# Attention stage with three banks for transposed probabilities, and feature products added up in the bank of attended values

## The chip, the cores and the metric

One core of one Trainium2 chip runs the whole program. The metric is the device time of one execution in microseconds. The kernel before took 2473.31 us (median of 3 runs, 2469.48 to 2473.86). Engines are called TensorE (PE in the profile; PEld is its weight load), VectorE (DVE), ScalarE (ACT), GpSimd (POOL) and SyncE (SP, which here only issues DMAs).

## The reference

x is 16 batch rows of 512 tokens with 128 values. Each row is layer-normalised, then `x + attention(xn) + ffn(xn)` is returned. The change lies wholly in the attention, which has 16 heads of width 8 and learned relative positions, clipped at 20 on both sides:

```python
idx = clip(pos[None, :] - pos[:, None], -20, 20) + 20
attn1 = einsum('bhqd,bhkd->bhqk', q, k)
attn2 = einsum('bhqd,qkd->bhqk', q, rel_k[idx])
attn = softmax((attn1 + attn2) / sqrt(8), axis=-1)
w1 = einsum('bhqk,bhkd->bhqd', attn, v)
w2 = einsum('bhqk,qkd->bhqd', attn, rel_v[idx])
out = (w1 + w2).transpose(0, 2, 1, 3).reshape(B, S, E) @ Wo.T + bo
```

w2 is computed from "features": for each query and head the probabilities of the 40 keys near it, as a 640-long vector, times a table made of rel_v. The second half of the sum, a small attention and a mixture of experts, is done by the two later stages, which the change leaves as they are.

## The kernel before, in words

Three stages follow each other: `attend`, `mix` and `experts`. Each is a block in which every engine runs its own list of instructions, written out by hand; engines meet at semaphores only. `attend` goes over 16 batch rows, and preparations for a row (normalising, q, k, v, splits into bf16 parts) are made two rows ahead (LEAD = 2) between the work of the row in hand.

A row has 16 **units** (u = 0 to 15). A unit has 4 score tiles of 128 x 512 (each for 32 queries of each of 4 heads), treated as two pairs. For a pair, TensorE makes the scores (L469) in the four-bank tensor b_s, VectorE adds the relative-position window (L644) and takes the negated maximum (L679), and ScalarE takes the exp with its sum (L818). One unit later TensorE transposes each tile of probabilities (L481, four products of 128 x 128 per tile) into one of two banks, b_pt. ScalarE reads tiles 0 and 2 (L792), VectorE tiles 1 and 3 (L661) into SBUF. Three units later TensorE multiplies them with v (L502, 16 instructions a unit) into the bank b_o, where the four 128-column quarters belong to the four tiles of 128 queries (t = u // 4). Per pair TensorE's order is scores, then (in the second pair) attended, then the transposes of the pair (`row`, L546 to 575).

The banks b_pt also take other jobs. JOBS (L74 to 78) lists all of them in order of unit; `bank_of` (L104) gives a job the bank of its index modulo 2, and `bank_free`, `job_done` and `job_read` (L217 to 227) count, from that list, what has to have happened before. So every job waits until the job two places before it has been read out. The other jobs are, after the four tiles of their unit:

- units 0, 4, 8, 12: `features` (L508): four transposes of feature chunks into one bank, the fifth into the next. ScalarE copies the four to feat_t (L830), VectorE the fifth to last_t (L701).
- units 3, 5, 6, 13: x transposed (L437, read at L755), q (L440, read by VectorE at L612), k (L440, read at L760) and v (L443, read at L782) of the row that is prepared.
- units 10, 11, 14, 15: the products with the relative-position table ("qr", L451), in two banks, read by ScalarE (L737, L738). The first waits for both banks (L447, L448).
- unit 9: the output product of the row before (L542, read at L836 and L715).

`weigh` (L522) multiplies the features with the table in units 1, 5, 9 and 13, for the features of t = (u // 4 - 2) % 4, so that t = 2 and 3 of a row fall into units 1 and 5 of the next. It uses a bank of its own, b_w. ScalarE copies b_o to o_sb in unit 2 of the next row (L824). When the fourth weigh is done, VectorE adds b_w to o_sb in unit 6 (L709, 128 x 512). Then GpSimd's `scale` (L989) adds the part of the far keys and multiplies by the inverse sums (L993, L995), GpSimd goes on with the row's next features (L906 to L926), and TensorE makes the output product in unit 9. In row 0, 20 warm-up products go to b_w in unit 3 (L563).

A start flag on a matmul clears the marks of its bank in the partitions that it writes; a product without the flag overwrites where the mark is clear and adds where it is set. Before, `attended` sets the flag on the first products of each quarter (hh == 0), and `weigh` on its first chunk. The file holds these flags as

```python
first = hh == 0
ins = nc.tensor.matmul(b_w[:, 0, t * P:(t + 1) * P], feat_w[:, c, :], ..., start=c == 0, stop=c == FC - 1)
```

Of the kernel before, what the change touches and what calls it, by code (L numbers as in the profile page):

```python
# [72 lines left out]
LEAD = 2  # L73
JOBS = [(u, "probs", j) for u in range(UNITS) for j in range(NJ)]  # L74
JOBS += [(u, "features", n) for u in range(0, UNITS, 4) for n in range(2)] + [(9, "out", n) for n in range(2)]
# [4 lines left out]
OF_ROW_BEFORE += [(9, "out", n) for n in range(2)]  # L80
# [14 lines left out]
def jobs_before(b, job, bank=None):  # L95

    def count(jobs):
        return sum(bank is None or JOBS.index(x) % 2 == bank for x in jobs)

    earlier = JOBS[:JOBS.index(job)]  # L100
    return sum(count(OF_ROW[n]) for n in range(-LEAD, b)) + count([x for x in earlier if x in OF_ROW[b]])


def bank_of(job):  # L104
    return JOBS.index(job) % 2
# [8 lines left out]
def attend(nc, w, scr):  # L114
# [11 lines left out]
    with ExitStack() as ctx:  # L126
# [52 lines left out]
        b_pt = [ps(f"pt{n}") for n in range(2)]  # L179
        b_o, b_w = ps("o"), ps("w")  # L180
# [13 lines left out]
        pt_ps, pt_ev = sem("pt_ps"), [sem("pt_ev0"), sem("pt_ev1")]  # L194
        av_ps, w_ps, o_ev, w_ev = sem("av_ps"), sem("w_ps"), sem("o_ev"), sem("w_ev")
# [224 lines left out]
        def _(pe):  # L420
# [65 lines left out]
            def attended(b, u, s):  # L486

                t, hh = u // 4, u % 4
# [7 lines left out]
                first = hh == 0  # L496
# [25 lines left out]
            def weigh(b, u):  # L522

                t = (u // 4 - 2) % NT
                for n in range(2):
                    job_read(pe, b, (u - 1, "features", n))
                if t == 0:
                    need(pe, w_ev, b, 1, 0)
                for c in range(FC):
                    ins = nc.tensor.matmul(b_w[:, 0, t * P:(t + 1) * P], feat_w[:, c, :],  # L530
                                           feat_t[:, c, :] if c < FC - 1 else last_t[:, t, :],
                                           start=c == 0, stop=c == FC - 1)
                ins.then_inc(w_ps, 1)
# [12 lines left out]
            def row(b, s, m, first=False, tail=False, lead=False):  # L546
# [5 lines left out]
                for u in range(10 if tail else UNITS):  # L552
                    if u == 0 and not tail:
                        pe.wait_ge(qk_in[s], m * QK_IN + QK_IN)
                    for pair in ((0, 1), (2, 3)):
                        if not tail:
                            scores(b, u, pair, s)
                        if pair[0]:
                            if u > 2 and not tail:
                                attended(b, u - 3, s)  # L560
                                if first and u == 3:

                                    warm_up(nc, b_w[:, 0, 0:P], ident[:], WARM)  # L563
                            elif u < 3 and not first:
                                attended(b - 1, u + UNITS - 3, 1 - s)
                        for j in pair:
                            if (u and not tail) or (u == 0 and not first):
                                transpose(b, u, j)
                    if u % 4 == 1 and not (first if u < 8 else tail):
                        weigh(b, u)  # L570
# [11 lines left out]
        def _(v):  # L582
# [81 lines left out]
            def row(b, s, m, first=False, tail=False, lead=False):  # L664
# [4 lines left out]
                for u in range(10 if tail else UNITS):  # L669
# [24 lines left out]
                    if u % 4 == 0 and not (first if u < 8 else tail):  # L694
                        job = (u, "features", 1)
                        t = (u // 4 - 2) % NT
                        job_done(v, b, job)
                        if t == 0:
                            need(v, w_ps, b, NT, 0)
# [5 lines left out]
                    if u == 6 and not first:  # L705

                        v.wait_ge(w_ps, b * NT)
                        v.wait_ge(o_ev, b)
                        nc.vector.tensor_tensor(o_sb[:], o_sb[:], b_w[:, 0, :].rearrange("p (t q) -> p t q", q=P),  # L709
                                                ALU.add).then_inc(w_ev, 1)  # L710
# [14 lines left out]
        def _(act):  # L725
# [69 lines left out]
            def row(b, s, m, first=False, tail=False, lead=False):  # L795
# [6 lines left out]
                for u in range(10 if tail else UNITS):  # L802
# [23 lines left out]
                    if u % 4 == 0 and not (first if u < 8 else tail):  # L826
                        job = (u, "features", 0)
                        job_done(act, b, job)
                        need(act, w_ps, b, NT, u // 4 - 2)
# [14 lines left out]
        def _(g):  # L844
# [144 lines left out]
            def scale(b):  # L989

                g.wait_ge(w_ev, b)
# [778 lines left out]
```

## Time and profile before

| what | value |
|---|---|
| median of 3 runs | 2473.31 us (2469.48 to 2473.86) |
| the profiled execution | 2466.72 us, its span 2464.9 us |
| TensorE busy | 2128.0 us (86%) |
| VectorE busy | 1864.7 us (76%) |
| ScalarE busy | 1619.9 us (66%) |
| GpSimd busy | 1030.4 us (42%) |
| DMA engines in the first stage | 54% |
| mean granted clock of TensorE | 0.961 |

The profile is of one execution. Busy time is the union of an engine's instructions; the time just before an instruction in which its engine was idle is shown in brackets, with what ended it. Instructions of the same kind that follow each other are merged into one line of the timeline with their count. The page's own chain of waits runs back from the end of the program and stays in the last stage, so it says nothing on the first.

### The profile page before, as it was taken

The numbers are of one execution on the slowest core, as the hardware profiler recorded it, in microseconds if no ns is written. First come the engines' busy times: TensorE is split into PE (matmuls) and PEld (weight loads), VectorE is DVE, ScalarE is ACT, GpSimd is POOL, SyncE is SP. The second block draws the span as 40 slices with busy tenths as digits, with TensorE's granted clock in tenths as the row PEclk, the third lists the DMA queues.
The fourth block names the chain that finished last, engine by engine and source line by source line (L and its number), as shares of the span: only waits on it lengthen the run. The fifth ranks groups of instructions, "written<-read, shape, count | busy, mean of one in ns | idle before, by whom it ended". The sixth has DMA issues, their size and how long they took to land. (4 is left out here: it accounts for less than half of the span.)

```text
span 2464.9 us, 77225 instructions
## 1 busy us (share of the span) xinstructions
PE 2128.0 (86%) x27816; PEld 1444.4 (59%) x27816; DVE 1864.7 (76%) x4151; ACT 1619.9 (66%) x4178; POOL 1030.4 (42%) x1270
## 2 busy tenths in 40 slices
PE   3388888888888888888888888599999978999999
PEld 1266566666666666666666666356666645666665
DVE  1388888888888888888888889367676756877777
ACT  2288888888888888888888878367777752323222
POOL 4246655655656656556655554200000003333332
PEclk7699999999999999999999999789999998999999
DMA  3355655555655655555555554200100110010110
GB/s 101 104 123 130 149 137 120 148 134 121 149 130 127 147 136 129 140 134 128 144 134 125 136 119 83 46 23 26 39 26 26 38 61 26 30 35 26 32 32 18
DMA packets 571232, 228.63 MB, mean 93 GB/s; under 512 B 465590, under 2 KB 543030, under 8 KB 566326
## 3 DMA queue, kind: packets, MB, share of 16 engines
q1 hardware_dynamic: 570934, 224.63, 36.8%
q8 instruction: 191, 3.13, 0.5%
q14 instruction: 107, 0.88, 0.1%
HBM read 129.61 MB, written 94.90 MB: 91 GB/s over the span
## 5 line engine op out<-in xcount | busy, mean ns | idle before, releaser
L818 ACT ACTIVATE a_probs<-a_bank_s,a_neg_max 128x512 f32<-128x512 f32 x1024 | 695.0, 685 | 134.0 <-DVE a_neg_max L679 131.0
L679 DVE TENSOR_REDUCE a_neg_max<-a_bank_s 128x2 f32<-128x1024 f32 x512 | 627.1, 1225 | 55.6 <-DVE a_bank_s L644 1.9
L481 PE MATMUL a_bank_pt<-a_ident,a_probs 128*128 128x128 f32 x4096 | 588.2, 284 | 64.8 <-ACT a_feat_t L830 42.9
L481 PEld LDWEIGHTS a_bank_pt<-a_ident,a_probs 128*128 128x128 f32 x4096 | 444.1, 143 | 201.0 <-issue 67.5
L792 ACT ACTIVATE a_probs_t<-a_bank_pt 128x512 f32<-128x512 f32 x512 | 306.0, 598 | 138.7 <-PE a_bank_pt L481 136.9
L661 DVE COPY a_probs_t<-a_bank_pt 128x512 f32<-128x512 f32 x512 | 349.7, 683 | 26.9 <-PE a_bank_pt L481 21.9
L502 PE MATMUL a_bank_o<-a_probs_t,a_v 128*32 128x128 f32 x8192 | 285.4, 281 | 1.4 <-issue 0.2
L644 DVE TENSOR_TENSOR a_bank_s<-a_bank_s,a_win 128x144 f32<-128x144 f32 (+2 forms) x640 | 161.3, 271 | 148.2 <-PE a_bank_s L469 145.3
L1537 ACT ACTIVATE e_gate<-e_bank_g 128x512 f32<-128x512 f32 x144 | 85.9, 597 | 273.9 <-PE e_bank_g L1476 273.9
L502 PEld LDWEIGHTS a_bank_o<-a_probs_t,a_v 128*32 128x32 f32 x8192 | 215.0, 112 | 58.1 <-issue 39.6
L937 POOL TENSOR_TENSOR a_win<-a_raw,a_band 128x1152 f32<-128x1152 f32 x64 | 168.9, 2639 | 105.2 <-issue 73.8
L1484 PEld LDWEIGHTS e_bank_y<-e_w,e_hid 128*128 128x128 f32 x1152 | 149.4, 192 | 95.2 <-issue 56.5
L818 ACT ACTIVATION_READ_ACCUMULATOR a_probs<-a_bank_s,a_neg_max 128x1 f32 x1024 | 203.7, 199 | 0.0
L1226 DVE TENSOR_REDUCE m_neg_max<-m_bank_s 128x2 f32<-128x1024 f32 x128 | 156.7, 1225 | 60.3 <-PE m_bank_s L1190 53.1
L1323 ACT ACTIVATE m_probs<-m_bank_s,m_neg_max 128x512 f32<-128x512 f32 x256 | 173.5, 683 | 13.4 <-DVE m_neg_max L1226 5.0
L469 PE MATMUL a_bank_s<-a_kl,a_q 48*32 48x204 bf16 (+14 forms) x3840 | 156.1, 275 | 20.3 <-ACT a_probs L818 20.0
L1199 PEld LDWEIGHTS m_bank_pt<-m_ident,m_probs 128*128 128x128 f32 x1024 | 112.4, 143 | 99.0 <-issue 82.7
L1289 POOL TENSOR_TENSOR m_rms<-m_rms,m_pows 128x4 f32<-128x4 f32 x16 | 16.1, 1008 | 368.8 <-DVE m_rms L1239 368.8
L1484 PE MATMUL e_bank_y<-e_w,e_hid 128*128 128x128 f32 x1152 | 156.0, 279 | 16.0 <-DVE e_hid L1646 16.0
L469 PE MATMUL a_bank_s<-a_k,a_q 48*32 48x512 bf16 (+15 forms) x4096 | 166.0, 289 | 0.0
L451 PE MATMUL a_bank_pt<-a_relx,a_t 64*128 64x320 f32 x256 | 62.1, 503 | 112.0 <-DVE a_probs_t L661 64.8
L1561 DVE SCALAR_TENSOR_TENSOR e_y<-e_bank_y,e_comb,e_y 128x128 f32<-128x128 f32 x512 | 143.9, 344 | 12.2
(163 smaller groups left out, 3489.7 us busy)
## 6 DMA issues: line engine op xcount, KB each, us to landing
scr_probs<-a_probs SPq DMA_DIRECT2D x512, 72.0 KB, 2.4
a_raw<-scr_qr SPq DMA_DIRECT2D x256, 96.0 KB
scr_qr<-a_qr SPq DMA_DIRECT2D x64, 320.0 KB, 3.6
a_feat<-scr_probs SPq DMA_DIRECT2D x256, 78.0 KB, 2.4
scr_parts<-a_sp SPq DMA_DIRECT2D x144, 128.0 KB, 2.4
a_left<-scr_probs SPq DMA_DIRECT2D x256, 64.0 KB, 2.5
a_q<-scr_parts SPq DMA_DIRECT2D x32, 192.0 KB
a_k<-scr_parts SPq DMA_DIRECT2D x32, 192.0 KB
```

Of the source, the lines that this page charges most:

```text
L469: ins = nc.tensor.matmul(b_s[g * QBLK:(g + 1) * QBLK, p, a:z], Q[s][par:par + ROWS, half, at:at + QBLK], keys[s][par:par + ROWS, half, a:z ...
L481: ins = nc.tensor.transpose(b_pt[bank_of(job)][:, 0, t * P:(t + 1) * P], probs[(u - 1) % 4][:, j, MAX_REL + t * P:MAX_REL + (t + 1) * P], ...
L502: ins = nc.tensor.matmul(out, V[s][:, V_SLOTS.index((edge, kt)), j, hh * 24:hh * 24 + 32], blocks[:, :, :, kt * P + j * QBLK:kt * P + (j + ...
L644: ins = nc.vector.tensor_tensor(near, near, bass.AP(own.tensor, own.offset, [own.ap[0], [step, n], [1, z - a]]), ALU.add)
L661: nc.vector.tensor_copy(probs_t[(u - 1) // 2 % 2][:, spot(u - 1, PLACES[j]), :], b_pt[bank_of(job)][:, 0, :]).then_inc(pt_ev[bank_of(job)], 1)
L679: nc.vector.tensor_reduce(neg_max[:, 2 * pair:2 * pair + 2], b_s[:, 2 * pair:2 * pair + 2, :], AX.X, ALU.max, negate=True).then_inc(max_ok, 1)
L792: nc.scalar.activation(probs_t[(u - 1) // 2 % 2][:, spot(u - 1, PLACES[j]), :], b_pt[bank_of(job)][:, 0, :], ACT.Copy).then_inc(pt_ev[bank ...
L818: nc.scalar.activation(probs[u % 4][:, j, MAX_REL:MAX_REL + S], b_s[:, j, :], ACT.Exp, bias=neg_max[:, j:j + 1], accum_out=sums[:, t, PLAC ...
L937: nc.gpsimd.tensor_tensor(win[t % 2][:], over, band[:].rearrange("p (o h c) -> p o h c", o=1, h=1) .to_broadcast([P, NQB, NJ, WIN]), ALU.m ...
L1226: nc.vector.tensor_reduce(neg_max[:, 2 * pair:2 * pair + 2], b_s[:, 2 * pair:2 * pair + 2, :], AX.X, ALU.max, negate=True).then_inc(max_ok, 1)
L1323: nc.scalar.activation(probs[:, j, :], b_s[:, j, :], ACT.Exp, bias=neg_max[:, j:j + 1], accum_out=sums[s][:, u, j:j + 1]).then_inc(exp_ok, 1)
L1484: ins = nc.tensor.matmul(b_y[k][:, t * P:(t + 1) * P], hid[k][:, t * P:(t + 1) * P], w2[:, e, :], start=True, stop=True)
```

## The change

The feature products of t = 0, 1 and 2 are added straight into b_o, in the quarter of their tile, with no start flag; only the very first attended products of a row (u == 0) have one. The products of t = 3 come when b_o already takes the next row; they go, as a new job WEIGHED at unit 5, to one of the b_pt banks, and VectorE adds that 128 x 128 part to o_sb at the end of unit 5. b_w is gone, and b_pt has three banks, given by the job's index modulo 3. ScalarE's guard on feat_t and GpSimd's guard in `scale` follow. The warm-up products go to b_o at the end of unit 2 of row 0.

```diff
 LEAD = 2
+PT_BANKS = 3
+WEIGHED = (5, "weigh", 0)
...
-JOBS += [(u, "features", n) for u in range(0, UNITS, 4) for n in range(2)] + [(9, "out", n) for n in range(2)]
+JOBS += [(u, "features", n) for u in range(0, UNITS, 4) for n in range(2)] + [WEIGHED] + [(9, "out", n) for n in range(2)]
...
 def bank_of(job):
-    return JOBS.index(job) % 2
+    return JOBS.index(job) % PT_BANKS
...
-        b_pt = [ps(f"pt{n}") for n in range(2)]
-        b_o, b_w = ps("o"), ps("w")
+        b_pt = [ps(f"pt{n}") for n in range(PT_BANKS)]
+        b_o = ps("o")
...
-                first = hh == 0
+                first = u == 0
...
-                if t == 0:
-                    need(pe, w_ev, b, 1, 0)
+                apart = t == NT - 1
+                if apart:
+                    bank_free(pe, b, WEIGHED)
+                out = b_pt[bank_of(WEIGHED)][:, 0, 0:P] if apart else b_o[:, 0, t * P:(t + 1) * P]
                 for c in range(FC):
-                    ins = nc.tensor.matmul(b_w[:, 0, t * P:(t + 1) * P], feat_w[:, c, :],
-                                           feat_t[:, c, :] if c < FC - 1 else last_t[:, t, :],
-                                           start=c == 0, stop=c == FC - 1)
-                ins.then_inc(w_ps, 1)
+                    ins = nc.tensor.matmul(out, feat_w[:, c, :], feat_t[:, c, :] if c < FC - 1 else last_t[:, t, :],
+                                           start=apart and c == 0, stop=c == FC - 1, skip_group_check=True)
+                ins.then_inc(pt_ps if apart else w_ps, 1)
...
-                                if first and u == 3:
-
-                                    warm_up(nc, b_w[:, 0, 0:P], ident[:], WARM)
...
+                    if first and u == 2:
+                        warm_up(nc, b_o[:, 0, 0:P], ident[:], WARM)
...
+                        if t == 0 and not first:
+                            job_done(v, b, WEIGHED)
                         if t == 0:
-                            need(v, w_ps, b, NT, 0)
                             need(v, att_ok, b, 1, 0)
...
-                    if u == 6 and not first:
-
-                        v.wait_ge(w_ps, b * NT)
+                    if u == 5 and not first:
+                        job_done(v, b, WEIGHED)
                         v.wait_ge(o_ev, b)
-                        nc.vector.tensor_tensor(o_sb[:], o_sb[:], b_w[:, 0, :].rearrange("p (t q) -> p t q", q=P),
-                                                ALU.add).then_inc(w_ev, 1)
+                        nc.vector.tensor_tensor(o_sb[:, NT - 1, :], o_sb[:, NT - 1, :], b_pt[bank_of(WEIGHED)][:, 0, 0:P],
+                                                ALU.add).then_inc(pt_ev[bank_of(WEIGHED)], 1)
...
-                        need(act, w_ps, b, NT, u // 4 - 2)
+                        if u != 8:
+                            need(act, w_ps, b, NT - 1, {0: -1, 4: 0, 12: 1}[u])
+                        elif not first:
+                            job_done(act, b, WEIGHED)
...
-                g.wait_ge(w_ev, b)
+                g.wait_ge(o_ev, b)
+                job_read(g, b, WEIGHED)
```

## Rows read from the trace of the kernel before

**Rows 1.** The stretches view of four parts of the span; busy us per engine, clock, DMA.
```profile
98.00:1576.00 1478.00, 1267.60 (x21800) 912.48 (x21782) 1236.83 (x2558) 1180.09 (x3023) 828.88 (x1138) 0.98 0.54 129
```

**Rows 2.** VectorE's add at L709, one per batch row: first and last start.
```profile
L709 DVE TENSOR_TENSOR a_o_sb<-a_o_sb,a_bank_w x16: 676/676/689, 226.9 to 1567.8; 128x512 f32<-128x512 f32 x16
```

**Rows 3.** The stretches view of fifteen pieces of 89.4 us, from 98 us on.
```profile
187.40:276.80 89.40, 77.25 (x1357) 55.45 (x1358) 75.99 (x160) 73.52 (x190) 51.82 (x69) 1.00 0.57 136
276.80:366.20 89.40, 77.09 (x1308) 55.06 (x1307) 75.05 (x157) 72.32 (x186) 53.19 (x74) 0.98 0.56 138
...
sum 1341.00, PE 1156.26 PEld 829.89 DVE 1129.54 ACT 1086.81 POOL 770.69; mean PE 77.08 PEld 55.33 DVE 75.30 ACT 72.45 POOL 51.38
```

**Rows 4.** The waits view from 700 to 1060 us: us in total, times, longest.
```profile
PE a_bank_pt L451 <- DVE a_probs_t L661: 18.4, 16, 1.4
...
PE a_bank_pt L481 <- ACT a_feat_t L830: 10.3, 15, 0.7
...
PE a_bank_pt L515 <- ACT a_probs_t L792: 7.2, 15, 0.8
...
PE a_bank_s L469 <- ACT a_probs L818: 3.3, 11, 0.3
```

**Rows 5.** VectorE's groups of instructions from 833 to 923 us: busy, mean ns, idle before.
```profile
L679 DVE TENSOR_REDUCE a_neg_max<-a_bank_s 128x2 f32<-128x1024 f32 x32 | 39.2, 1225 | 3.4
...
L644 DVE TENSOR_TENSOR a_bank_s<-a_bank_s,a_win 128x144 f32<-128x144 f32 (+2 forms) x40 | 10.1, 271 | 6.7 <-PE a_bank_s L469 6.6 <-DVE a_y_in L715 0.2
...
L701 DVE COPY a_last_t<-a_bank_pt 128x128 f32<-128x128 f32 x4 | 1.2, 292 | 1.7 <-PE a_bank_pt L519 1.7
...
L612 DVE TENSOR_SCALAR a_t<-a_bank_pt,a_bias_q 128x512 f32<-128x512 f32 x1 | 0.8, 751 | 0.7 <-PE a_bank_pt L440 0.7
```

**Rows 6.** The timeline of all engines in unit 10: start, us, instruction, idle before.
```profile
799.04 1.09 PE L481 MATMUL a_bank_pt<-a_ident,a_probs 128*128 128x128 f32 x8
...
800.03 0.59 ACT L792 ACTIVATE a_probs_t<-a_bank_pt 128x512 f32<-128x512 f32 x1
...
800.73 0.68 DVE L661 COPY a_probs_t<-a_bank_pt 128x512 f32<-128x512 f32 x1
...
801.55 0.90 PE L451 MATMUL a_bank_pt<-a_relx,a_t 64*128 64x320 f32 x4 [1.42 <-DVE a_probs_t L661]
...
802.87 0.32 DVE L644 TENSOR_TENSOR a_bank_s<-a_bank_s,a_win 128x144 f32<-128x144 f32 x1 [1.46 <-PE a_bank_s L469]
```

**Rows 7.** The timelines of TensorE and VectorE around unit 12's features.
```profile
812.64 0.63 PE L515 MATMUL a_bank_pt<-a_ident,a_feat 128*128 128x128 f32 x4 [0.40 <-ACT a_probs_t L792]
...
814.75 1.09 PE L481 MATMUL a_bank_pt<-a_ident,a_probs 128*128 128x128 f32 x8 [0.70 <-ACT a_feat_t L830]
...
813.74 0.29 DVE L701 COPY a_last_t<-a_bank_pt 128x128 f32<-128x128 f32 x1 [0.42 <-PE a_bank_pt L519]
```

**Rows 8.** The timelines of TensorE and VectorE in units 3 to 6.
```profile
865.16 0.39 PE L530 MATMUL a_bank_w<-a_last_t,a_feat_w 128*128 128x128 f32 x2
...
870.77 1.13 PE L440 MATMUL a_bank_pt<-a_xnt,a_wk 128*128 128x512 f32 x2 [0.49 <-ACT a_probs_t L792]
...
855.13 0.32 DVE L644 TENSOR_TENSOR a_bank_s<-a_bank_s,a_win 128x144 f32<-128x144 f32 x1 [0.29 <-PE a_bank_s L469]
...
866.44 0.75 DVE L612 TENSOR_SCALAR a_t<-a_bank_pt,a_bias_q 128x512 f32<-128x512 f32 x1 [0.68 <-PE a_bank_pt L440]
...
871.42 0.68 DVE L709 TENSOR_TENSOR a_o_sb<-a_o_sb,a_bank_w 128x512 f32<-128x512 f32 x1
872.31 0.32 DVE L644 TENSOR_TENSOR a_bank_s<-a_bank_s,a_win 128x144 f32<-128x144 f32 x1 [0.22 <-PE a_bank_s L469]
```

**Rows 9.** GpSimd's timeline, the end of unit 8's feature chain.
```profile
880.42 0.22 POOL L926 TENSOR_TENSOR a_feat<-a_left 128x16 f32<-128x16 f32 x1
```

**Rows 10.** Stretches of 3 us, and TensorE's timeline, behind unit 14.
```profile
827.00:830.00 3.00, 3.00 (x44) 2.19 (x46) 2.54 (x5) 2.51 (x6) 1.88 (x2) 0.50 0.91 160
...
826.61 1.94 PE L481 MATMUL a_bank_pt<-a_ident,a_probs 128*128 128x128 f32 x8
```

More of the change, by code:

```diff
@@ L79 @@
 OF_ROW_BEFORE = [(0, "probs", j) for j in range(NJ)] + [(u, "features", n) for u in (0, 4) for n in range(2)]
-OF_ROW_BEFORE += [(9, "out", n) for n in range(2)]
+OF_ROW_BEFORE += [WEIGHED] + [(9, "out", n) for n in range(2)]
 def of_row(b):
@@ L97, in count @@
     def count(jobs):
-        return sum(bank is None or JOBS.index(x) % 2 == bank for x in jobs)
+        return sum(bank is None or bank_of(x) == bank for x in jobs)
     earlier = JOBS[:JOBS.index(job)]
@@ L193, in attend @@
         s_ps, max_ok, exp_ok = sem("s_ps"), sem("max_ok"), sem("exp_ok")
-        pt_ps, pt_ev = sem("pt_ps"), [sem("pt_ev0"), sem("pt_ev1")]
-        av_ps, w_ps, o_ev, w_ev = sem("av_ps"), sem("w_ps"), sem("o_ev"), sem("w_ev")
+        pt_ps, pt_ev = sem("pt_ps"), [sem(f"pt_ev{n}") for n in range(PT_BANKS)]
+        av_ps, w_ps, o_ev = sem("av_ps"), sem("w_ps"), sem("o_ev")
         p_out = [sem(f"p_out{k}") for k in range(4)]
```

## The prediction

> **What bounds the kernel now.** I read the stretches first, then the waits inside the attention stage, then short pieces of each engine's timeline.
>
> The change touches the first of three stages, from about 98 to 1576 us of a span of 2464.9 us [rows 1]; what follows has the same instructions before and after and only starts earlier. The 16 batch rows follow each other at (1567.8 - 226.9) / 15 = 89.4 us [rows 2]. Of such a stretch TensorE is busy 77.1 us, VectorE 75.3, ScalarE 72.5 [rows 3]. No engine is full; three engines hand 64 banks of transposed probabilities to each other in a row. So the reader has to ask, wait by wait, who is late.
>
> From 700 to 1060 us, which is 4.03 rows, the largest waits of TensorE are on the two pt banks [rows 4]: 16 waits of the products for the relative-position table (L451, "QR" below) on VectorE's copy of the last transposed tile, 18.4 us; 15 waits of the first transposes after the features on ScalarE's copy of the features, 10.3 us; 15 of the feature transposes (L515) on ScalarE's copy of a tile, 7.2 us. Per row that is 4.6 + 2.6 + 1.8 us; with the smaller ones of the same kind, for x, q and k, about 10.3.
>
> Not all of this is on the path. VectorE's idle time shows what is [rows 5]: in one row it waits 6.7 us ahead of the window add (L644), most of it in the second half of the row, 1.7 us ahead of the copy of the last feature chunk (L701), 0.7 ahead of the q copy (L612). Its 3.4 us ahead of L679 have no releaser: they are the delay from an add to the maximum of its result, 0.11 us each, and stay. In units 0 to 9 VectorE works almost without a gap, and TensorE's bank waits are mostly absorbed; in units 9 to 15 they are passed on to VectorE nearly one for one.
>
> **The change, part by part.** With three banks a job waits for the reader of the third job before it, not of the second. JOBS has 87 entries, a multiple of 3, so the rotation closes at each row and no job's wait on a pt bank gets stricter.
>
> **QR products, units 10, 11, 14, 15.** The first waits for both banks. Today the later of the two holds the last tile of the unit, read by VectorE; afterwards it holds the tile before, read by ScalarE. In unit 10 ScalarE ends at 800.03 + 0.59 = 800.62 us, VectorE at 800.73 + 0.68 = 801.41, and the products start at 801.55 [rows 6]: 0.79 us to gain, as TensorE's own transposes end before (799.04 + 1.09 = 800.13). The same subtraction gives 0.67, 0.83 and 0.53 us in units 11, 14 and 15: 2.8 us a row. VectorE then sits idle 1.46 us for the scores behind it [rows 6], so this is on the path. A part comes back: the second tile of the next unit now waits for ScalarE's read of the first QR bank, which stands behind two exps and hardly moves. Today both tiles wait for it, so the second half of that unit gains one tile's time, 1.09 / 2 = 0.54, where the first half gained 0.8. I take 0.6 each, **2.4 us a row** (ends 2.0 and 2.8).
>
> **Features, units 0, 4, 8, 12.** The four transposes need no ScalarE copy any more (they wait 0.40 us in unit 12), so the fifth, and with it VectorE's copy behind its 0.42 us of idle, comes about 0.4 us earlier [rows 7]. The first tile after them no longer waits 0.70 us for the feature copy; the second does, and gains 0.5. 0.45 each, **1.8 us a row** (ends 1.2, where VectorE's backlog absorbs a third, and 2.4).
>
> **x, k and the big add (units 3, 5, 6).** x: VectorE's 0.29 us of idle behind it [rows 8], **0.3**. At unit 6 today's add of 128x512 takes 0.68 us of VectorE, while TensorE's k product has waited 0.49 us for a bank, and VectorE then idles 0.22 us for the scores [rows 8]. Both leave together: **0.6** (ends 0.2 and 0.9). The new add of 128x128 stands at unit 5. Its price from the nearest row, the 128x128 copy from a bank, is 0.29 us [rows 7]. It waits for the weigh of the last tile, which ends at 865.16 + 0.39 = 865.55 us; VectorE idles 0.68 us until 866.44, for a q product that TensorE issues after the weigh anyway [rows 8]. So it costs nothing while that gap holds; without the cover it costs its 0.3 us and the wait for the weigh. Queued behind it are the q copy and the next window add.
>
> **At nothing.** The weigh products keep count and kind; whether start is on shows in no row as a difference, L502 has both. The v products (unit 13) and the output product (unit 9) come on TensorE right behind weigh, without a bank wait; VectorE's gaps there are TensorE's own work and stay. The warm-up moves up by about one unit in the first row only, at the same cost; I bound the effect at 2 us either way. GpSimd's scaling starts some 5 us earlier, as its releaser moves up from unit 6 to 5. Today the feature chain behind it ends at 880.42 + 0.22 = 880.64 us [rows 9], about when TensorE could transpose: it would be late next in a faster row, and is relieved. After that comes the load of left, which in the three other places leaves several us. SyncE's queue issues the same DMAs in the same order.
>
> **The clock.** Once in most rows TensorE's granted clock falls to 0.50 (1.2 GHz; elsewhere 2.4) for some 3 us, right after unit 14's QR wait [rows 10]: 8 transposes take 1.94 us instead of 1.09, and a full 3 us at half speed is 1.5 us of work lost. 11 of the 15 stretches stand at 0.98, three at 1.00 [rows 3]. If all dips go that is 17 us; if none, 0. The wait ahead of them shrinks to under 0.5 us, but unit 10's longer wait has no dip behind it, so the wait alone doesn't decide. I take 10 us.
> The Trainium skill ("TensorE: Matmul & The Clock Gate", section "A second HAM failure mode: psum-queue depth-cycling") blames small idle gaps of TensorE between groups for such a clock. By it all dips would go, 17 us in place of 10; the trace agrees on their place, not on which gap brings them.
>
> **Sum.** 2.4 + 1.8 + 0.3 + 0.6 = 5.1 us a row. x, k and QR are there in the 14 rows that prepare another: 71 us. The two last rows have features and add only: 2 x 2.3 = 5. The stage's tail has the add on its last chain, 0.68 against 0.3: 0.4. With the clock's 10: 86 us. The profiled execution took 2466.7 us around its span of 2464.9; the median of three runs is 2473.3, 0.3% more, and I take the difference over to it: **2387 us**.
>
> **The rivals.**
> *A, VectorE and ScalarE set the pace.* What TensorE gains comes back as waits on exps, of which it has 3.3 us in 4.03 rows today [rows 4]: ScalarE has the QR reads and the splits on top of its exps in units 10 to 15. Then half of QR (1.2) and the features of three units (0.4 x 3) stay, and 0.5 for the add: 2.9 x 14 + 5 = 45 us, 2428 us. For it: units 0 to 9 are like that. Against: the 6.7 us that VectorE waits are on TensorE's scores, not on ScalarE. Chance 0.22.
> *B, all bank waits go.* 10.3 us a row in 14 rows, 144 us: 2329 us. Against: VectorE's idle time is no longer than that, and part of it is TensorE's own work. Chance 0.09.
> The Trainium skill ("Perfetto Trace Analysis", section "Optimizing Tensor Performance") says to rotate independent groups through banks so that evacuation overlaps the next group. Taken alone it gives B.
> *C, no change.* The banks are not the limit: the QR products start a fixed delay after the transposes. Rows 6 speak against it, with 1.42 us between. 2473 us, chance 0.05.
> *D, slower: the clock.* TensorE gets ahead of VectorE, works in short bursts, waits on exps, and the clock falls more often. A dip costs 1.5 us: from 5.1 / 1.5 = 3.4 extra dips a row on, the gain is gone. With five more a row it loses 7.5 - 5.1 = 2.4 us in 14 rows, 34, less the last rows' 5: 2502 us. Against: in units 0 to 9 TensorE waits on exps already, and one whole row holds 1.00 [rows 3]. Chance 0.05.
> *Forecast:* chance 0.59.
>
> **How the numbers follow.** About 0.2%, 5 us, is what a measurement of this kernel can tell from no change. Forecast, A and B are on the fast side: 0.90; C 0.05; D 0.05. The forecast's own bounds: low ends 2.0 + 1.2 + 0.2 + 0.2 = 3.6 a row, 50 + 5, clock 0: 55 us, 2418; high ends 2.8 + 2.4 + 0.3 + 0.9 = 6.4, 90 + 5 + 17: 112 us, 2361. The range goes down to 2345, halfway to B, and up to 2432, over A; left out are C, D and most of B, under 0.2.
>
> **What would show it.** The pitch of the rows down from 89.4 to about 84 us. The QR products released by ScalarE's copy (L792) after under 0.7 us, no more by L661. No wait of the feature transposes for a tile copy; the wait for the feature copy on the second tile, near 0.1 us. VectorE's idle ahead of the window add near 4 us a row instead of 6.7. The 128x128 add without idle that outlasts the weigh. More stretches at 1.00. It would be wrong if TensorE's scores waited on exps by 3 us a row (A), or if stretches at 0.50 multiplied (D).

## The result, and the profile after

The kernel after took 2433.09 us (median of 4 runs, 2432.04 to 2443.62), the kernel before beside it 2471.39 us (4 runs, 2469.14 to 2473.86). The ratio is 0.9854, 95% interval 0.9825 to 0.9884: 38 us gained where 86 were forecast, and 1 us outside the range. The profiled execution of after is the slowest of its four, 2443.6 us, so its trace shows 23 us less than the profiled one of before.

The stretch of the first stage, and the small add that ends each row's sum, both of the kernel after:

```profile
98.00:1553.00 1455.00, 1260.99 (x21800) 921.34 (x21784) 1225.48 (x2560) 1154.80 (x3024) 829.30 (x1138) 0.96 0.55 131
```

```profile
L712 DVE TENSOR_TENSOR a_o_sb<-a_o_sb,a_bank_pt x16: 227/230/287, 217.9 to 1543.9; 128x128 f32<-128x128 f32 x16
```

The row pitch is (1543.9 - 217.9) / 15 = 88.4 us, against 89.4 [rows 2] and 84.3 forecast. The granted clock of the stage is 0.96, against 0.98 [rows 1]. The two later stages take 454 and 435 us in both kernels. So the whole shortfall lies in the rows.

The waits of the whole stage after (engine, what it was about to do, what released it: us in total, times, longest):

```profile
DVE a_bank_s L647 <- PE a_bank_s L471: 102.8, 71, 52.7
...
DVE a_probs_t L664 <- PE a_bank_pt L483: 72.6, 35, 6.3
...
PE a_bank_pt L483 <- ACT a_qr L741: 49.0, 14, 6.3
ACT a_qr_first L740 <- issue: 45.0, 14, 6.0
PE a_bank_pt L483 <- ACT a_feat_t L836: 41.1, 61, 0.7
PE a_bank_s L471 <- ACT a_probs L821: 39.1, 94, 3.1
...
PE a_bank_pt L453 <- ACT a_probs_t L795: 23.3, 47, 2.0
...
DVE a_last_t L705 <- PE a_bank_pt L522: 15.2, 16, 8.1
```

The same view of the kernel before, those lines that answer to them and do not stand in rows 4:

```profile
DVE a_bank_s L644 <- PE a_bank_s L469: 145.3, 99, 52.8
...
PE a_bank_pt L451 <- DVE a_probs_t L661: 64.8, 56, 1.4
PE a_bank_pt L481 <- ACT a_feat_t L830: 42.9, 62, 0.7
DVE a_last_t L701 <- PE a_bank_pt L519: 35.3, 64, 8.4
PE a_bank_pt L515 <- ACT a_probs_t L792: 31.1, 60, 0.8
...
DVE a_probs_t L661 <- PE a_bank_pt L481: 21.9, 24, 4.3
```

Most bank waits changed as forecast. The QR products (now L453) wait 23.3 us for ScalarE instead of 64.8 for VectorE, and the first four feature transposes no longer wait for a tile. VectorE's idle time ahead of the window add fell by 145.3 - 102.8 = 42.5 us, ahead of the last feature chunk by 20.1. But a wait that was not there before stands on ScalarE, at its read of the QR bank (L740): 45.0 us, once a row, up to 6.0 us long. "issue" here means that no engine released it. TensorE then waits 49.0 us for that read, and VectorE's idle time ahead of L664 grew by 72.6 - 21.9 = 50.7 us. The balance of VectorE: -42.5 - 20.1 + 50.7, less 16 x (676 - 230) ns = 7.1 us for the smaller add, is 19 us of the 23.

What L740 waits for shows in unit 14 of one row, after: the timeline of SyncE, ScalarE and TensorE (start, us, instruction, idle before), and below it the QR store among the DMAs issued from 800 to 815 us (KB each, median us from issue to landing).

```profile
798.71 0.38 SPq L341 DMA_DIRECT2D scr_qr<-a_qr  x1
...
802.14 0.43 SPq L252 DMA_DIRECT2D a_x<-in_x  x1
802.67 3.00 SPq L341 DMA_DIRECT2D scr_qr<-a_qr  x1
...
807.92 0.93 PE L453 MATMUL a_bank_pt<-a_relx,a_t 64*128 64x320 f32 x4 [0.45 <-ACT a_probs_t L795]
...
811.40 0.18 ACT L740 ACTIVATE a_qr_first<-a_bank_pt 128x8 f32<-128x8 f32 x1 [1.91 <-issue]
...
811.96 0.66 PE L483 MATMUL a_bank_pt<-a_ident,a_probs 128*128 128x128 f32 x4 [2.18 <-ACT a_qr L741]
```

```profile
scr_qr<-a_qr SPq DMA_DIRECT2D x1, 320.0 KB, 8.7
```

ScalarE copies the QR products of a row's four tiles into two SBUF buffers in turn, and SyncE stores each. Ahead of its copy both kernels have this wait (t is the tile, n the row):

```python
need(act, out_qr, n, 16 * NT, 16 * 2 * (t // 2))
```

One semaphore, out_qr, counts all QR stores that have landed, 16 for each; `need` waits until it stands at n * 64 plus the last argument. For the third tile (t = 2, unit 14) that is two more than at the row's start: both stores that the row has issued so far. The first, at 798.71, reads the buffer that L740's instructions are about to overwrite; it landed after 4.3 us, at 803.0. The second, at 802.67, reads the other buffer and lands 8.7 us later, at 811.4, which is when L740 starts. So it is in all 14 rows: L740 starts within 0.12 us of the landing of the second store, and 7.3 to 9.0 us after that of the first. The wait is on a store that does not use the buffer. A semaphore for each of two buffers would not ask for it; no run has that. In the kernel before, the same store and read:

```profile
815.92 3.88 SPq L339 DMA_DIRECT2D scr_qr<-a_qr  x1
...
826.05 0.18 ACT L737 ACTIVATE a_qr_first<-a_bank_pt 128x8 f32<-128x8 f32 x1
```

```profile
scr_qr<-a_qr SPq DMA_DIRECT2D x1, 320.0 KB, 9.6
```

It landed at 815.92 + 9.6 = 825.5 and was asked for at 826.05: 0.5 us to spare, the least of the 14 rows, where it is 0.5 to 4.8 us. After, the copy in the row shown is ready 811.40 - 1.91 - 802.67 = 6.8 us behind the store's issue, before it was 10.1 us. A faster row does not bring the store forward by as much: from its loads of left in unit 9 to this store SyncE issues nearly without a pause in both kernels, for 16.5 to 19.4 us before and 15.3 to 18.5 us after.

### The profile page after: what moved, and what is told of

It is laid out like the page before. It is cut to its first block and busy times, and to the rows that moved or that the text cites. A ratio compares the mean times of both kernels' runs of the same rounds, so it can differ in the third digit from the quotient of the medians.

```text
span 2441.8 us, 77225 instructions
## 1 busy us (share of the span) xinstructions
PE 2122.4 (87%) x27816; PEld 1453.6 (60%) x27816; DVE 1852.5 (76%) x4151; ACT 1594.5 (65%) x4178; POOL 1030.8 (42%) x1270
## 5 line engine op out<-in xcount | busy, mean ns | idle before, releaser
L483 PE MATMUL a_bank_pt<-a_ident,a_probs 128*128 128x128 f32 x4096 | 597.3, 286 | 103.5 <-ACT a_qr L741 49.0
L483 PEld LDWEIGHTS a_bank_pt<-a_ident,a_probs 128*128 128x128 f32 x4096 | 449.3, 144 | 237.1 <-issue 94.4
L664 DVE COPY a_probs_t<-a_bank_pt 128x512 f32<-128x512 f32 x512 | 350.2, 684 | 78.2 <-PE a_bank_pt L483 72.6
L647 DVE TENSOR_TENSOR a_bank_s<-a_bank_s,a_win 128x144 f32<-128x144 f32 (+2 forms) x640 | 161.3, 271 | 106.1 <-PE a_bank_s L471 102.8
L821 ACT ACTIVATION_READ_ACCUMULATOR a_probs<-a_bank_s,a_neg_max 128x1 f32 x1024 | 212.3, 207 | 0.0
L923 POOL TENSOR_TENSOR a_left<-a_left,a_keep 128x512 f32<-128x512 f32 x64 | 81.6, 1275 | 296.9 <-DMA a_left<-scr_probs 296.9
L471 PE MATMUL a_bank_s<-a_kl,a_q 48*32 48x204 bf16 (+14 forms) x3840 | 157.0, 276 | 39.6 <-ACT a_probs L821 39.1
L471 PEld LDWEIGHTS a_bank_s<-a_kl,a_q 48*32 48x32 bf16 x3840 | 60.1, 89 | 160.5 <-issue 147.0
```

Of the source, the lines that this page charges most:

```text
L471: ins = nc.tensor.matmul(b_s[g * QBLK:(g + 1) * QBLK, p, a:z], Q[s][par:par + ROWS, half, at:at + QBLK], keys[s][par:par + ROWS, half, a:z ...
L483: ins = nc.tensor.transpose(b_pt[bank_of(job)][:, 0, t * P:(t + 1) * P], probs[(u - 1) % 4][:, j, MAX_REL + t * P:MAX_REL + (t + 1) * P], ...
L647: ins = nc.vector.tensor_tensor(near, near, bass.AP(own.tensor, own.offset, [own.ap[0], [step, n], [1, z - a]]), ALU.add)
L664: nc.vector.tensor_copy(probs_t[(u - 1) // 2 % 2][:, spot(u - 1, PLACES[j]), :], b_pt[bank_of(job)][:, 0, :]).then_inc(pt_ev[bank_of(job)], 1)
L821: nc.scalar.activation(probs[u % 4][:, j, MAX_REL:MAX_REL + S], b_s[:, j, :], ACT.Exp, bias=neg_max[:, j:j + 1], accum_out=sums[:, t, PLAC ...
```

## The experiments

All times are medians; "before" is the kernel before on the same chip. It differs by up to 6 us between the groups of runs, so a difference across groups is given against each group's own before too, where that matters.

| run | us | before | ratio, 95% |
|---|---|---|---|
| after, QR store ahead of x (1) | 2417.1 | 2466.7 | 0.9801, 0.9782 to 0.9820 |
| before, same order (1) | 2467.6 | 2466.7 | 1.0000, 0.9988 to 1.0013 |
| third bank for WEIGHED only (2) | 2464.6 | 2466.7 | 0.9998, 0.9986 to 1.0010 |
| after, three QR buffers (3) | 2426.6 | 2467.9 | 0.9827, 0.9799 to 0.9855 |
| before, three QR buffers (3) | 2469.8 | 2467.9 | 1.0003, 0.9987 to 1.0018 |
| three buffers, QR waits as before (3) | 2425.0 | 2467.9 | 0.9821, 0.9782 to 0.9860 |
| three buffers, features wait as before (3) | 2428.6 | 2467.9 | 0.9824, 0.9788 to 0.9859 |
| three buffers, no q and k loads (4) | 2363.3 | 2470.4 | 0.9563, 0.9547 to 0.9579 |
| three buffers, short q and k loads (4) | 2362.8 | 2470.4 | 0.9560, 0.9544 to 0.9576 |
| before, no q and k loads (4) | 2465.0 | 2470.4 | 0.9973, 0.9963 to 0.9983 |
| no loads, QR waits as before (5) | 2399.8 | 2470.4 | 0.9711, 0.9694 to 0.9727 |
| no loads, features wait as before (5) | 2401.4 | 2473.0 | 0.9718, 0.9701 to 0.9734 |
| after (1), early q and k (6) | 2509.7 | 2473.0 | 1.0151, 1.0134 to 1.0168 |
| three buffers, early q and k (6) | 2509.4 | 2473.0 | 1.0154, 1.0135 to 1.0173 |
| before, early q and k (6) | 2525.8 | 2473.0 | 1.0226, 1.0205 to 1.0247 |
| after (1), q and k at the gap (7) | 2480.3 | 2468.9 | 1.0049, 1.0030 to 1.0068 |
| after (1), q and k in two gaps (7) | 2481.8 | 2468.9 | 1.0055, 1.0037 to 1.0073 |
| three buffers, two gaps (7) | 2489.2 | 2468.9 | 1.0083, 1.0059 to 1.0106 |

**1. The QR store ahead of the load of x.** In unit 12 SyncE issues the 256 KB load of the next x just ahead of the QR store that turned out late. Exchanged, in the kernel after and in the one before:

```diff
+                if u in (11, 12, 15):
+                    store_qr(b, (11, 12, 15).index(u))
                 if u == 12 and n + 1 < B:
...
                     load_x(n + 1)
-                if u in (11, 12, 15):
-                    store_qr(b, (11, 12, 15).index(u))
```

> The changed kernel, with the store of the second QR buffer issued ahead of the load of x in unit 12, on the same queue. Theory S (the changed kernel loses in unit 14, where ScalarE's QR read waits for that store, which lies behind the 256 KB load of x): ScalarE's 45 us of waits ahead of the QR read at L740 and TensorE's 49 us behind it nearly vanish, and the time falls from 2433 to 2385 to 2400 us. Rival L (SyncE's queue is late as a whole, or the DMA engines are full, so the order inside it doesn't matter): waits and time stay, 2425 to 2435. Rival V (VectorE's chain sets the pace and takes over): the waits vanish but the time stays over 2420, with more waits on exps.

> The kernel before, with the same reorder of store and load. Theory S: there the store lands before the read asks for it, so nothing changes, 2466 to 2476 us. Rival L: the same. If the load of x were late for its own reader instead, it would be slower than 2476.

Sixteen us faster after (2417.1 against 2433.1; 11 us against each one's own before), where theory S said 33 at the least; nothing before. ScalarE's wait for the store after the exchange:

```profile
ACT a_qr_first L740 <- issue: 25.6, 8, 4.5
```

The wait fell from 45.0 to 25.6 us and is not gone. Ahead of the load the store still lands 7.8 to 9.6 us after its issue (7.6 to 9.7 behind it), and in 13 of the 14 rows the copy still starts within 0.12 us of the landing. One of those that are left, with TensorE's line behind it, and the stretches around it (the last three numbers are clock, DMA share and GB/s):

```profile
796.12 1.11 PE L483 MATMUL a_bank_pt<-a_ident,a_probs 128*128 128x128 f32 x4 [4.72 <-ACT a_qr L741]
...
797.72 1.93 PE L505 MATMUL a_bank_o<-a_probs_t,a_v 128*32 128x128 f32 x32
```

```profile
792.00:796.00 4.00, 0.00 (x0) 0.00 (x0) 0.54 (x1) 0.44 (x3) 0.00 (x0) 0.71 0.26 70
796.00:800.00 4.00, 3.88 (x54) 2.66 (x55) 2.18 (x4) 2.80 (x9) 1.39 (x2) 0.50 0.79 129
```

TensorE does nothing for 4 us, then runs the next 4 us at 0.50, that is 1.2 GHz: the 32 products take 1.93 us, 1.08 at full speed. The stall of 4.7 us so costs nearly 2 us more behind it.

**2. The third bank for WEIGHED alone.** The feature products go to b_o and WEIGHED has a bank to itself; all other jobs keep two.

```diff
 def bank_of(job):
-    return JOBS.index(job) % PT_BANKS
+    if job == WEIGHED:
+        return 2
+    return (JOBS.index(job) - (JOBS.index(job) > JOBS.index(WEIGHED))) % 2
```

> The changed kernel, but the third bank is used for the weighed job alone and all others alternate between two banks as before. Theory: this has only the small add at unit 5 in place of the large one at unit 6, worth about 0.4 to 0.6 us a row: 2460 to 2468 us, and TensorE's waits for banks are those of before (QR on VectorE's copy 65 us). Rival (the gain comes from the add and the earlier scaling, not from the banks): near 2433.

```profile
PE a_bank_pt L455 <- DVE a_probs_t L666: 65.6, 56, 1.4
...
PE a_bank_pt L520 <- ACT a_probs_t L797: 31.7, 61, 0.8
```

The bank waits are those of before, and so is the time, within 3.5 us faster to 2.5 slower. The smaller add, the earlier scaling and the moved warm-up bring nothing that can be measured; the gain of the change is the rotation's.

**3. A third QR buffer.** Three SBUF buffers for QR rows, each with a semaphore of its own, so that the copy waits for the store of its own buffer alone. Room for it comes from two slots instead of four for last_t and sums and from a broadcast column of ones, with the waits that these need.

```diff
-        QR = [sb(f"qr{k}", [P, H, FAR]) for k in range(2)]
+        QR = [sb(f"qr{k}", [P, H, FAR]) for k in range(3)]
...
-                    need(act, out_qr, n, 16 * NT, 16 * 2 * (t // 2))
+                    need(act, out_qr[(NT * n + t) % 3], (NT * n + t) // 3, 16, 0)
```

> The changed kernel with a third buffer for the QR rows, so that ScalarE's read in unit 14 waits for a store of three reads ago and not of two (room for it from two slots instead of four for the last feature chunk and for the sums, and one column of ones broadcast). Nothing of the computation is left out. Theory S (the loss is the wait for the QR store's landing): the waits ahead of ScalarE's QR read in the rows go to 0 from 45 us, and with them the slow clock behind them; 2380 to 2400 us. Rival V (VectorE's chain takes over): the waits go, but the time stays at 2410 or more, near the run with only the reorder (2417), and TensorE waits more on exps.

> The kernel before with the same third QR buffer. Theory S: the store was never late there, so 2462 to 2472 us, no difference. If the slots or the broadcast cost something by themselves, it shows here as slower.

Nothing before. Against after it is 7 us, and 3 us with each against its own before, where the intervals overlap: little or nothing. The waits with three buffers:

```profile
POOL a_left L929 <- DMA a_left<-scr_probs: 347.7, 47, 11.6
...
PE a_bank_pt L457 <- ACT a_probs_t L801: 55.5, 55, 3.9
...
PE a_bank_pt L522 <- POOL a_feat L938: 32.6, 20, 4.7
...
ACT a_probs L827 <- DMA scr_probs<-a_probs: 22.9, 12, 3.4
```

The wait on the QR store is gone, by the third buffer or by the semaphores, which this run does not tell apart. Others stand in its place, again on DMAs: GpSimd waits 347.7 us for the load of left (161.7 before, 296.9 after), the feature transposes 32.6 us for GpSimd, and the exps for the stores of probabilities whose buffer they overwrite. On top of this kernel the QR products, and then the features, were made to wait for the same reads as before:

```diff
                         if job[2] == 0:
                             bank_free(pe, b, (u, "qr", 1))
+                            if b >= 0:
+                                job_read(pe, b, (u, "probs", 3))
```

```diff
                 bank_free(pe, b, job)
+                if (u, "probs", 2) in OF_ROW[b]:
+                    job_read(pe, b, (u, "probs", 2))
                 for c in range(FC - 1):
```

(the same for the fifth transpose with tile 3, and for the first two tiles after them with the feature copies.)

> As the run with three QR buffers, but the QR products wait, as in the kernel before, also for VectorE's read of the last tile of the unit. The prediction's term is 2.4 us in 14 rows: 34 us slower than with three QR buffers (28 to 39 by its ends). Rival A (ScalarE and VectorE set the pace there): 17 us or less.

> As the run with three QR buffers, but around the features the waits of the kernel before are kept: the four transposes wait for ScalarE's read of tile 2, the fifth for VectorE's of tile 3, and the first two tiles of the next unit for the reads of the feature banks. The prediction's term is 1.8 us in 16 rows: 29 us slower (19 to 38). Rival: VectorE's backlog absorbs it, under 10 us.

Neither costs anything: 2425.0 and 2428.6 against 2426.6, each inside the spread of the runs. What TensorE gains at one place it waits for at the next. Something else paces the row at about this time.

**4. The bytes of q and k.** Each row prepares the next by 18 loads of q and k from the scratch, in units 3 to 12. Left out from the third row on, so that the rows compute with stale q and k:

```diff
-                        load_qk(b + 1, 1 - s, STACK[done:done + SPREAD[u]])
+                        if b == 0:
+                            load_qk(b + 1, 1 - s, STACK[done:done + SPREAD[u]])
...
-                        pe.wait_ge(qk_in[s], m * QK_IN + QK_IN)
+                        pe.wait_ge(qk_in[s], QK_IN)
```

and, in a second kernel, all 18 issued but each with an eighth of its bytes.

> As the run with three QR buffers, but the 18 loads of q and k per row are left out from the third row on, which then computes with what rows 0 and 1 loaded. This leaves out DMA work only; every engine's own instructions stay. Theory D (the changed kernel is now held by SyncE's queue and its DMAs, whose stores of probabilities and loads of features come late): without them 2380 to 2400 us, ScalarE's waits on stores (23 + 17 us) and TensorE's on the features (33 us) nearly gone. Rival V (VectorE's and ScalarE's chains are the limit): 2415 or more.

> As the run with three QR buffers, but the 18 loads of q and k per row keep their count and shrink to an eighth of their bytes from the third row on (stale q and k are computed with). Theory D1 (the issuing of SyncE's queue, in order, is the limit): like three QR buffers, 2415 to 2435. Theory D2 (the bytes on the 16 DMA engines, behind which the stores land late): like the run without these loads, 2380 to 2400.

> The kernel before without the same 18 loads per row. Theory D: there DMA was hidden, so at most 5 us come off: 2460 to 2470. If it falls by 20 us or more, the loads themselves cost time in both kernels, by another way than the one named.

Without these bytes the change, with its third QR buffer, brings 2465.0 - 2363.3 = 101.7 us. The loads cost the kernel before 5 us and the one with three QR buffers 63 (66 with each against its own before). The eighth of the bytes gives the same 2362.8, so it is bytes and not the issuing. The kernel without the loads:

```profile
PE a_bank_s L476 <- ACT a_probs L828: 35.5, 91, 0.7
PE a_bank_pt L458 <- ACT a_probs_t L802: 24.5, 56, 0.6
POOL a_left L930 <- DMA a_left<-scr_probs: 22.6, 13, 8.6
```

```profile
98.00:1480.00 1382.00, 1229.71 (x21758) 900.29 (x21757) 1218.59 (x2550) 1151.22 (x3020) 823.53 (x1134) 0.99 0.51 114
```

```profile
L719 DVE TENSOR_TENSOR a_o_sb<-a_o_sb,a_bank_pt x16: 226/228/288, 206.9 to 1461.7; 128x128 f32<-128x128 f32 x16
```

The load of left is waited for 22.6 us in place of 347.7, the clock is 0.99, and the pitch is (1461.7 - 206.9) / 15 = 83.7 us, forecast 84.3. The DMA engines' mean share hardly differs, 0.51 against 0.55: a mean says nothing on when a transfer lands. Scores wait on exps here (35.5 us) nearly as after (39.1), in a kernel 70 us faster; so that wait is not what paces after.

**5. The two main terms, without the loads.** The two edits of 3 on the kernel without the loads.

> As the run without the loads of q and k, with the QR products waiting for VectorE's read of the last tile as before. Theory D: now that DMA no longer hides it, the prediction's term shows: 25 to 39 us slower than without this wait. Rival V: under 10 us slower, as with the loads (where the two were equal).

> As the run without the loads of q and k (2363 us), with the waits around the features as in the kernel before. The prediction's term is 1.8 us in 16 rows: 29 us slower, 2392 (19 to 38 by its ends). Rival: VectorE's backlog absorbs it, under 10 us.

```profile
PE a_bank_pt L460 <- DVE a_probs_t L671: 72.0, 56, 1.4
```

```profile
PE a_bank_pt L527 <- ACT a_probs_t L808: 41.8, 63, 1.0
```

Each brings the waits of before back. The QR waits cost 2399.8 - 2363.3 = 36.5 us, the features' 2401.4 - 2363.3 = 38.1 (35.4 with each against its own before).

**6. All loads of q and k earlier.** If the loads disturb the QR stores of units 11 to 15, they might go ahead of them.

```diff
-        SPREAD = [0, 0, 0, 2, 2, 2, 2, 2, 2, 1, 2, 2, 1, 0, 0, 0]
+        SPREAD = [0, 0, 0, 3, 3, 2, 3, 3, 3, 1, 0, 0, 0, 0, 0, 0]
```

> The changed kernel, complete, with the store of the QR rows ahead of the load of x in unit 12 and the 18 loads of q and k issued in units 3 to 9 instead of 3 to 12, out of the stretch with the large stores. Theory D2 (bytes in flight in units 10 to 14 make the stores of probabilities and of QR rows land late): 2380 to 2400 us. Rival (the bytes matter wherever they are; moved forward they delay the features' loads of units 5 and 9): 2410 to 2430, with more of TensorE's waits on the features.

> The same with three buffers for QR rows. Theory D2: a little below the run before it, 2368 to 2395 us, as the store of a QR row then has more time. Rival: no difference to it, or the 2427 of the three buffers alone.

> The kernel before with the loads of q and k in units 3 to 9. Theory D2: DMA is hidden there, 2464 to 2474 us, no difference. If it gains 10 us or more, the new place helps by another way.

Ninety-three us slower than the first kernel of 1 (86 with each against its own before), and the kernel before loses 53, where theory D2 said no difference. The gain that it gave for the changed kernel and the rival's 2410 to 2430 us are missed too; only that the third buffer adds nothing came true. TensorE's wait for the QR reads fell to 2.4 us in the first of the three, but there are:

```profile
PE a_bank_pt L518 <- POOL a_feat L932: 63.6, 23, 5.2
...
PE a_bank_pt L453 <- ACT a_probs_t L795: 51.7, 56, 2.8
ACT a_probs L821 <- DMA scr_probs<-a_probs: 43.8, 25, 5.5
```

The features and the stored probabilities are late instead. In the kernel before with early loads the feature transposes wait 41.7 us for GpSimd, where they waited 7.9.

**7. The loads beside the idle stretch.** While SyncE waits for landed probabilities in units 5, 9 and 13 the DMA engines have least to do, so loads were issued ahead of it.

```diff
-        SPREAD = [0, 0, 0, 2, 2, 2, 2, 2, 2, 1, 2, 2, 1, 0, 0, 0]
+        SPREAD = [0, 0, 0, 2, 2, 2, 2, 2, 2, 3, 1, 1, 1, 0, 0, 0]
...
+                    qk_first = u in (5, 9, 13) and not tail and not last
+                    if qk_first:
+                        done = sum(SPREAD[:u])
+                        load_qk(b + 1, 1 - s, STACK[done:done + SPREAD[u]])
                     if u % 4 == 1 and not (first if u == 1 else tail):
                         read_features(b, u)
```

(the second and third with 3 loads in unit 13 and none in 10 to 12.)

> Nothing is left out. The kernel after with the QR store ahead of the load of x in unit 12, and the 18 loads of q and k of a row placed anew: those of units 5, 9 and 13 are issued ahead of SyncE's wait for the landed probabilities instead of behind it, and unit 9 takes 3 of them where it took 1; units 10, 11 and 12 take 1 each instead of 2, 2 and 1. Theory 'the bytes in flight at the wrong time' (what a row loses is the delay of the QR stores and feature loads by the q and k loads beside them): the traces show the DMA engines least busy right behind unit 9's wait, so these bytes collide with less, and units 10 to 12 are relieved by 2 loads of 5: 2417 us of the same kernel without it comes down to 2395 to 2412. Rival 'order of issue': a load issued ahead of the wait is ahead of the feature load in the queue and delays it by as much as it relieves the stores: 2415 to 2435. Rival 'earlier is always worse', as the last early schedule was: above 2440.

> Nothing is left out. As the one before, but units 10, 11 and 12 take no load of q or k at all, and unit 13 takes 3, ahead of its wait. The last loads are then 1 unit later than today. Theory 'the bytes in flight at the wrong time': the QR stores of units 11 and 12 pass nearly alone, and this gains more than the one before: 2385 to 2405. Rival 'the loads themselves become late': the next row's scores begin on them at unit 0, three units on; with a load taking some 9 us and a unit 5.2 this should not show, but if it does TensorE waits at the row's start and the time is above 2417. Rival 'order of issue': unit 13's feature load comes later by three loads, and VectorE and TensorE wait for GpSimd: 2415 to 2440.

> Nothing is left out. The schedule of the one before on the kernel with three QR buffers (2427 us with the old schedule and store order). If what is left is the QR buffer's wait for its store, this is faster than the one before by 5 us and more; if it is the feature loads or the wait of the exps for stored probabilities, the two are within 5 us of each other.

63 to 72 us slower than 2417; the rival "order of issue" had the mechanism, and its numbers were too small. Three QR buffers did not help this schedule (2489.2 against 2481.8), so the QR store is not what holds it. The waits of the first:

```profile
POOL a_left L927 <- DMA a_left<-scr_probs: 425.6, 46, 16.0
...
PE a_bank_pt L522 <- POOL a_feat L936: 93.0, 28, 6.1
...
PE a_bank_pt L487 <- ACT a_qr L745: 3.6, 14, 0.8
```

and SyncE's timeline in unit 9, where three loads of q and k now stand ahead of the feature loads, with TensorE's next feature transposes:

```profile
800.56 2.15 SPq L274 DMA_DIRECT2D a_kl<-scr_parts  x3
805.90 5.62 SPq L304 DMA_DIRECT2D a_left<-scr_probs  x4
811.57 4.09 SPq L310 DMA_DIRECT2D a_feat<-scr_probs  x4
...
819.08 1.12 PE L522 MATMUL a_bank_pt<-a_ident,a_feat 128*128 128x128 f32 x4 [4.90 <-POOL a_feat L936]
```

The same unit in the first kernel of 1:

```profile
769.36 2.35 SPq L304 DMA_DIRECT2D a_left<-scr_probs  x4
771.75 2.34 SPq L310 DMA_DIRECT2D a_feat<-scr_probs  x4
...
777.81 0.60 PE L518 MATMUL a_bank_pt<-a_ident,a_feat 128*128 128x128 f32 x4
```

The QR store is in time, and the feature chain is late: with q and k just ahead of them the feature loads take 5.62 + 4.09 = 9.7 us to issue instead of 4.7, and TensorE waits 4.9 us for what GpSimd makes of them. Its transposes then take 1.12 us instead of 0.60, at a granted clock of 0.50 from 819 to 822 us.

## Why the prediction was right or wrong

**The QR products were right**: released by ScalarE's copy, after 0.45 us in unit 14, and worth 36.5 us where 34 were forecast, once the loads are out of the way. With them in, undoing this part costs nothing, and its gain is given back.

**The features were right in place and undersized**: 35 to 38 us against 1.8 x 16 = 29, at its high end of 2.4 x 16 = 38. The tile waits went, as forecast. That the wait for the feature copy would shrink to 0.1 us was wrong, it is 41.1 / 61 = 0.67 us; the gain shows ahead of the last feature chunk, 35.3 down to 15.2 us.

**The add was oversized.** It costs 0.23 us, with idle ahead of it only once, as forecast; but experiment 2 puts it and the earlier scaling under 3.5 us in all. x and k were not tried by themselves. Undoing the two main parts costs 75 us at most; the rest of the 101.7 is not assigned to any part.

**What failed is a sentence of "At nothing":** "SyncE's queue issues the same DMAs in the same order." That is true, and I let it stand for their cost. What hid them was slack between a landing and its use, and that was not named as a cover. The first to be late is a QR store, with 0.5 to 4.8 us of slack in the trace of before, where a landing of 9.6 us and the read could both be seen. I looked past it because nothing waited there, and did not read the wait itself, which asks for one store more than the buffer needs. In the trace of after it costs ScalarE 45.0 us and TensorE 49.0 us behind it. Behind it stand the load of left, of which I wrote that it "leaves several us", and the exps' wait for stored probabilities. When the wait on the store is removed, they take its place.

**The clock's sign was wrong:** 10 us were forecast as gain and the clock fell from 0.98 to 0.96; no piece of the length of a row stands at 1.00, where three did. TensorE's waits on readers of the pt banks, without the QR read, halved from 160 to 80 us, and stalls of 2 to 6 us on landings came, some with a stretch at 0.50 behind them. Without the loads it is 0.99, a gain as forecast.
The rule of the Trainium skill ("TensorE: Matmul & The Clock Gate", section "A second HAM failure mode: psum-queue depth-cycling") would have had all dips go with the small gaps. Taking half of the gaps away did not raise the clock while the long stalls stood, and with 56 of them put back in the kernel without the loads (experiment 5) it stayed at 0.99: on this point the traces do not agree with the rule.

**The rivals.** A's 2428 us is the number nearest to 2433, for another reason: scores' waits on exps did grow, from 20.0 to 39.1 us, but they are 35.5 us in the kernel that takes 2363 us. B stays too high even in the relieved kernel, 102 us against 144, with bank waits left there. C and D's verdicts did not come. D's mechanism, more time at half clock, did come, through stalls and not through bursts.

So of 101.7 us that the change brings with the loads' bytes gone, 38 are left. That the bytes take the rest is shown. With each run against its own before, they cost 66 us with three QR buffers, that buffer is worth 3, and 5 of the bytes' cost is in the kernel before too: 66 + 3 - 5 = 64. That no placing of them could get it back is not: three schedules were tried, all worse than the given one. Not tried with the given schedule were the reordered store together with the third QR buffer, two QR buffers with a semaphore each, and issuing part of the DMAs from another engine than SyncE. The best complete kernel is the reordered one, 2417.1 us.

## What to carry to other kernels

When a change shortens a loop, list every DMA by issue, landing and first use, and compare the smallest slack with what the change takes out; a transfer without a wait may be half a microsecond from having one. Read what each wait on a landing counts: one semaphore for two buffers can make an engine wait for the store of the buffer that it does not need. When undoing either of two gains costs nothing, a second bound holds the time: find it by taking bytes away, not by removing the next wait. Before moving a load to where the engines are idle, look at what is queued behind it.

## What was not expected of the hardware

- The 320 KB store of unit 12 landed 7.6 to 10.0 us after its issue in the 28 rows of before and after, where the median over the stage is 4.7 us, with the mean share of the DMA engines at 0.55. Ahead of the 256 KB load instead of behind it, it still took 7.8 to 9.6 us.
- Bytes, not issues: with the same 18 issues and an eighth of the bytes the time was 2362.8 us, without the issues 2363.3.
- The same q and k bytes cost 5 us in the kernel before, 63 in the faster one, and another 53 to 93 when moved by a few units.
- A TensorE stall of 4.7 us was followed by 4 us at 0.50, while 56 QR waits of up to 1.4 us, in the kernel without the loads and with the QR waits of before, go with a clock of 0.99 over its stage (98 to 1516 us), the same as without them.
